# A decoder layer in FP32: regrouping the attention heads on the partitions, and who copies, casts and stores around them

## The chip, the core and the metric

One core of a Trainium2 chip runs the whole program. Its engines work side by side, each through its own list of instructions, and wait for one another at semaphores: TensorE (PE in the profile; PEld is its weight loading), VectorE (DVE), ScalarE (ACT), GpSimd (POOL), and SyncE (SP), which here only issues DMA transfers. The metric is the time of the program on the device in microseconds (us), the median of several runs.

## What is computed

A post-norm decoder layer for 8 sequences of 128 tokens, width 128, 16 heads of 8: self attention with learned relative position logits, causal cross attention, a routed mixture of 64 experts (8 chosen) with a shared expert; after each a residual and a layer norm.

```python
x = layernorm(x + attn(x, qkv_w, qkv_b, proj_w, proj_b, rel_emb))
#   logits = q k^T / sqrt(8) + pos,   pos[i, j] = q_i . rel_emb[j - i + 99], -1e8 outside
#   softmax, times v, times proj_w^T, + proj_b
x = layernorm(x + cross(x, ctx, wq, wk, wv, wo))      # the same without pos, causal
x = layernorm(x + routed(x) + relu2(x @ shared_up_w) @ shared_down_w)
#   routed: sigmoid scores, best 4 of 8 groups, best 8 experts, weights normed, x 2.5
#   each expert: relu(x @ up)^2 @ down
```

## The kernel before

**Preparation.** A list of tasks (`TASKS`) goes through seven PSUM banks in a ring: TensorE computes a task into a bank, ScalarE or VectorE (`by_vector`) copies it out, and only then may the task seven places later use the bank. The tasks transpose the weights and `x`, project queries and keys (`q0`, `q1`, `k0`, `k1`: halves of the tokens), transpose the relative embeddings (`rel`), make values (`v0`, `v1`) and the same of the context (`ctx0`, `ctx1`, `vc0`, `vc1`), then the router's weights, then 32 `bias` tasks of four products each (256 matmul records): for every query position one product of `rel_t` with `spread`, the queries laid out once per head through a mask (`spread_queries`, VectorE, four batches of 16 instructions, L1086; the mask is `head_mask`). They give the position logits `pos`. Last come the context's keys, `kc0` and `kc1`.

**High and low parts.** Scores are products of FP32 values split in two reduced parts each, high (`q_hi`, `k_hi`) and low (`q_lo`, and `k_t` after it is overwritten with its own low part). GpSimd makes both in halves of the tokens (L528 to L535). So that one matmul over 128 rows sums all four products of parts (high and low by high and low) of four heads with 8 dimensions each, SP stores the parts to DRAM (`keep`, L398) as often as they are needed, and `gather(B)` loads for sequence B (0 to 7 self attention, 8 to 15 cross attention) a stack of queries, `q_stk` (one DMA, L413), and a block-diagonal `k_bd` (four DMAs, one for each of the four heads, L417). Three stacks form a ring (`RING`); gather B waits until the scores of sequence B-3 are done, and in the cross attention also for the store of its own queries, `qc_kept`. Before, the features on the partitions are ordered by `(h d g)`: four blocks of heads `h`, 8 dimensions `d`, four groups `g` innermost. The store's DRAM tensor has the shape (4, 4 parts, 32, tokens).

**The pipeline.** From there each engine runs a loop over steps `s`, and each step does a piece of each stage. Attention is cut into 64 units U (16 sequences x 4 groups g; 32 and up are cross attention). `scores(U)` adds the logits (L700: `pos` transposed; L703: the causal mask) and the product L706; VectorE takes the negative maxima (L1123), ScalarE four exponentials (L916), TensorE transposes the probabilities two steps later (L718), then either VectorE (L1130) or ScalarE (L925) copies them, by `probs_by_vector(U)`, and TensorE multiplies with the values (L728). Output projection, residual, layer norm and the next queries follow at fixed distances. In steps 34 and 38 VectorE also splits the first two pieces of expert weights; GpSimd does the others, and SP loads them (`load_piece`).

The experts run as 68 steps k (k = s - 67): 34 for the first half of the tokens (two shared, 32 pairs of experts), 34 for the second. A step is three products up (L683, high and low parts), a `scaled` on VectorE (ReLU times the root of the expert's weight, L1262), two squares on ScalarE (L992, L993), a subtraction on GpSimd (`unit_lo`, L594), and four steps later three products down. The routing is cut into 14 parts for each of four batches of two sequences; `BATCHES` and `ROUTE0` say in which step which part goes onto VectorE. `CT` are the two steps in which TensorE turns the finished weights `root` (L796); ScalarE copies them out, SP stores them to `root_dram` and loads them back spread over 64 rows each (`roots`).

Of the kernel before, what the change touches and what calls it, by code (L numbers as in the profile page):

```python
# [21 lines left out]
H, HD = 16, 8  # L22
# [50 lines left out]
CT = [ROOTS_AT[1], ROOTS_AT[3] + 2]  # L73
# [48 lines left out]
def probs_by_vector(U):  # L122

    return U % 4 != 3 if U < NU else U % 2 == 0
# [13 lines left out]
def decoder_layer(nc, x, ctx_in, qkv_w, qkv_b, proj_w, proj_b, rel_emb, wq, wk, wv, wo,  # L138
                  router_w, corr, up_w, down_w, sh_up, sh_down, out):
    with ExitStack() as ctx:  # L140
# [30 lines left out]
        with ExitStack() as second:  # L171
# [125 lines left out]
        k_kept = [sem(f"k_kept{n}") for n in range(2)]  # L297
        q_kept = [sem(f"q_kept{n}") for n in range(2)]
# [74 lines left out]
        def _(sp):  # L373
# [21 lines left out]
            def keep(store, parts, cols, kept):  # L395

                for part, what in enumerate(parts):
                    sp.dma_start(store[:, part, :, cols], what[:, cols]).then_inc(kept, 16)  # L398

            def keep_queries(store, hi, lo, cols, kept):  # L400
                keep(store, (hi, lo, hi, lo), cols, kept)

            def keep_keys(store, hi, lo, cols, kept):
                keep(store, (hi, hi, lo, lo), cols, kept)

            def gather(B):
# [933 lines left out]
```

## Time and profile before

| | us |
|---|---|
| median of 3 runs | 346.91 |
| lowest, highest | 346.52, 347.46 |
| the profiled execution | 344.19 |
| its span | 342.4 |
| busy: PE, DVE, ACT, POOL | 267.5, 228.3, 207.3, 141.0 |

The span is the time between the first and the last instruction of the profiled execution. Busy times are sums over the span, of engines that work beside each other. In the timelines a row is one instruction or a run of like ones ("x16"), and the square brackets give the engine's idle time just before and what ended it.

### The profile page before, as it was taken

How to read it: one execution, taken by the hardware profiler on the slowest of the kernel's cores; microseconds unless marked ns; L12 is line 12 of the kernel's file. 1: busy time of each engine (PE TensorE's matmuls, PEld its weight loads, DVE VectorE, ACT ScalarE, POOL GpSimd, SP SyncE). 2: the span in 40 equal slices, each digit the busy share in tenths (PEclk: the TensorE clock that was granted, in tenths of full speed). 3: DMA queues.
4: the chain of work that ended last, by engine and by line, in shares of the span. 5: the costliest groups of instructions: out<-in, count | busy, mean ns of one | idle time of the engine just before them, and what ended most of it. 6: DMA issues, size and time to landing. Idle time of an engine off the chain costs nothing.

```text
span 342.4 us, 6024 instructions
## 1 busy us (share of the span) xinstructions
PE 267.5 (78%) x1904; PEld 210.6 (62%) x1904; DVE 228.3 (67%) x571; ACT 207.3 (61%) x573; POOL 141.0 (41%) x139
## 2 busy tenths in 40 slices
PE   2919999893069999998778775649969599999991
PEld 2608999572057887665555443538747488878870
DVE  2697854663038888986659989449999745674533
ACT  1502362774018888898767863346666578878861
POOL 7560000600000012244443500227569589879990
PEclk9976999998569999999989987688989899999997
DMA  6522225733432333465554100099547267658501
GB/s 113 144 97 104 102 103 180 172 83 130 154 105 64 94 94 92 93 158 149 149 167 136 50 0 3 15 225 253 138 124 171 73 163 179 174 160 215 142 0 31
DMA packets 55683, 41.09 MB, mean 120 GB/s; under 512 B 15394, under 2 KB 44772, under 8 KB 55652
## 3 DMA queue, kind: packets, MB, share of 16 engines
q1 hardware_dynamic: 55652, 40.71, 43.7%
q8 instruction: 15, 0.25, 0.3%
q14 instruction: 16, 0.13, 0.1%
HBM read 31.52 MB, written 9.18 MB: 119 GB/s over the span
## 4 chain that ended last, share of the span: by engine, by line
PE 41%; DVE 18%; SPq 12%; DMA 11%; issue 7%; POOL 5%; ACT 4%; POOLq 0%; DVEq 0%; ACTq 0%
PE bank L683 14%; PE bank L667 9%; SPq L417 6%; DMA qc_dram<-q_lo 5%; POOL unit_lo L594 5%; PE bank L718 4%; PE bank L700 4%; DVE spread L1086 3%; SPq L398 2%; DMA k_bd<-k_dram 2%; SPq L413 2%; PE bank L728 2%; DVE scaled L1262 2%; PE bank L706 2%; PE bank L739 1%
## 5 line engine op out<-in xcount | busy, mean ns | idle before, releaser
L594 POOL TENSOR_TENSOR unit_lo<-unit,unit_hi 128x512 fp32r<-128x512 f32 x68 | 87.3, 1303 | 48.7 <-ACT unit_hi L993 47.5
L916 ACT ACTIVATE probs<-bank,neg_max 128x128 f32<-128x128 f32 x256 | 72.3, 390 | 29.1 <-DVE neg_max L1123 28.1
L1262 DVE SCALAR_TENSOR_TENSOR scaled<-bank,roots 128x512 f32<-128x512 f32 x64 | 43.4, 686 | 30.2 <-PE bank L683 22.5
L1123 DVE TENSOR_REDUCE neg_max<-bank 128x4 f32<-128x512 f32 x64 | 42.9, 683 | 29.6 <-PE bank L706 29.0
L992 ACT ACTIVATE unit<-scaled 128x512 f32<-128x512 f32 x68 | 42.7, 628 | 32.8 <-DVE scaled L1262 30.5
L718 PE MATMUL bank<-ident,probs 128*128 128x128 f32 x256 | 39.9, 279 | 3.3 <-DVE probs_t L1130 2.4
L993 ACT ACTIVATE unit_hi<-scaled 128x512 fp32r<-128x512 f32 x68 | 41.9, 616 | 0.0
L718 PEld LDWEIGHTS bank<-ident,probs 128*128 128x128 f32 x256 | 30.5, 145 | 10.5 <-issue 5.2
L561 POOL CAST q_hi<-q_t 128x128 fp32r<-128x128 f32 x8 | 2.3, 293 | 83.6 <-ACT q_t L963 83.6
L706 PE MATMUL bank<-k_bd,q_stk 128*128 128x512 f32 x64 | 34.6, 540 | 0.0
L1130 DVE COPY probs_t<-bank 128x512 f32<-128x512 f32 x40 | 27.5, 687 | 10.4 <-PE bank L718 9.7
L700 PE MATMUL bank<-ident,pos 128*128 128x128 f32 x128 | 20.5, 283 | 17.4 <-DMA k_bd<-k_dram 17.4
L683 PE MATMUL bank<-unit_hi,w_hi 128*128 128x512 f32 x64 | 26.6, 415 | 3.8 <-POOL unit_lo L594 3.8
L667 PE MATMUL bank<-spread,rel_t 128*128 128x128 f32 x256 | 29.3, 278 | 0.0
L1086 DVE TENSOR_SCALAR spread<-q_t,head_mask 128x256 f32<-128x256 f32 x64 | 25.0, 466 | 6.3 <-ACT q_t L883 3.3
L667 PEld LDWEIGHTS bank<-spread,rel_t 128*128 128x128 f32 x256 | 29.1, 194 | 0.1
L700 PEld LDWEIGHTS bank<-ident,pos 128*128 128x128 f32 x128 | 14.6, 143 | 21.4 <-issue 19.9
L683 PE MATMUL bank<-x_hi,w_hi 128*128 128x512 f32 x64 | 26.6, 415 | 0.1
L683 PE MATMUL bank<-x_hi,w_lo 128*128 128x512 f32 x64 | 25.9, 405 | 0.0
L683 PE MATMUL bank<-unit_lo,w_hi 128*128 128x512 f32 x64 | 25.7, 401 | 0.0
L683 PE MATMUL bank<-x_lo,w_hi 128*128 128x512 f32 x64 | 25.7, 401 | 0.0
L683 PE MATMUL bank<-unit_hi,w_lo 128*128 128x512 f32 x64 | 25.6, 400 | 0.0
(176 smaller groups left out, 480.6 us busy)
## 6 DMA issues: line engine op xcount, KB each, us to landing
roots<-root_dram SPq DMA_DIRECT2D x64, 256.0 KB, 4.6
q_stk<-q_dram SPq DMA_DIRECT2D x8, 256.0 KB, 3.6
k_bd<-k_dram SPq DMA_DIRECT2D x32, 64.0 KB, 3.0
incoming<-in_L_ffn_up_w SPq DMA_DIRECT2D x4, 512.0 KB, 5.3
q_stk<-qc_dram SPq DMA_DIRECT2D x8, 256.0 KB, 3.0
k_bd<-kc_dram SPq DMA_DIRECT2D x32, 64.0 KB, 2.4
incoming<-in_L_ffn_down_w SPq DMA_DIRECT2D x4, 512.0 KB, 4.8
q_dram<-q_hi SPq DMA_DIRECT2D x4, 256.0 KB
```

What stands on the lines that cost most here:

```text
L594: nc.gpsimd.tensor_tensor(unit_lo[:, k % R], unit[:, k % 3], unit_hi[:, k % R], ALU.subtract).then_inc(lo_ready, 1)
L667: last = nc.tensor.matmul(bank_of(f"bias{n}")[:, m * 128:(m + 1) * 128], rel_t[:, L - 1 - i:2 * L - 1 - i], q_spread[:, i // 32 % 2, i % 3 ...
L683: ins = nc.tensor.matmul(bank, w[a], act[b], start=(first and n == 0), stop=(last and n == 2), skip_group_check=True)
L700: nc.tensor.matmul(bank[:, h4 * L:(h4 + 1) * L], pos[:, row, :], ident[:, :], start=(h4 == 0), stop=False, is_transpose=True, skip_group_c ...
L706: nc.tensor.matmul(bank[:, :], q_stk[r][:, g, :], k_bd[r][:, g].rearrange("p h j -> p (h j)"), start=False, stop=True, skip_group_check=Tr ...
L718: last = nc.tensor.transpose(ps[BP][:, h4 * L:(h4 + 1) * L], probs[:, U % 3, h4 * L:(h4 + 1) * L], ident[:, :])
L916: last = nc.scalar.activation(probs[:, U % 3, h4 * L:(h4 + 1) * L], ps[BS[U % 3]][:, h4 * L:(h4 + 1) * L], ACT.Exp, bias=neg_max[:, U % 4, ...
L992: nc.scalar.activation(unit[:, k % 3], scaled[:, k % 3], ACT.Square)
L993: nc.scalar.activation(unit_hi[:, k % R], scaled[:, k % 3], ACT.Square).then_inc(hi_ready, 1)
L1086: last = nc.vector.tensor_scalar(q_spread[:, c % 2, :, h * NB:(h + 1) * NB], src, head_mask[:, h:h + 1], None, ALU.mult)
L1123: nc.vector.tensor_reduce(neg_max[:, U % 4, :], ps[BS[U % 3]][:, :].rearrange("p (h j) -> p h j", h=GH), AX.X, ALU.max, negate=True).then_ ...
L1262: ins = nc.vector.scalar_tensor_tensor(scaled[:, k % 3], h, 0.0, roots[:, n % ROOT_RING, c % ROOTS], ALU.max, ALU.mult)
```

## The change

- **Order of features.** On the partitions the heads are now innermost: `(d h)`, 8 dimensions by 16 heads. Weights, biases, relative embeddings and the head mask are permuted to that. `k_bd` rows of one head are every fourth partition (`h4::GH`) instead of 32 in a row.
- **Stores.** `keep` stores a part as 128 plain rows. Queries are stored once for the high and once for the low part (before: twice each), keys still twice each. The self attention's stores are no longer in halves of the tokens. A gather loads the query stack in two DMAs of 64 rows.
- **Order on SP.** Gather 2 comes ahead of the two first pieces of weights; the stores of the context's keys come after gathers 3 and 4 instead of ahead of gather 3.
- **High parts.** ScalarE makes `q_hi` and `k_hi` of the self attention, all tokens in one instruction each, ahead of its copies of the bias tasks. GpSimd waits for the first two batches of `spread`, then subtracts.
- **Probabilities.** In the cross attention VectorE copies one unit in four, ScalarE three; before, each copied two.
- **Routing.** The third batch of two sequences takes 12 steps instead of 8, the fourth starts at step 84 instead of 80; the weights of the second half are turned at step 96 instead of 93, one step after the last part of the routing instead of two.

```diff
-BATCHES = [(range(0, 2), 2), (range(2, 4), 3.5), (range(4, 6), 1.75), (range(6, 8), 1.2)]
+BATCHES = [(range(0, 2), 2), (range(2, 4), 3.5), (range(4, 6), 1.2), (range(6, 8), 1.2)]
 ROUTE0 = [NG * (NB + seqs[-1]) + M + USE + 2 for seqs, _ in BATCHES]
+ROUTE0[3] += NG
...
-CT = [ROOTS_AT[1], ROOTS_AT[3] + 2]
+CT = [ROOTS_AT[1], ROOTS_AT[3] + 1]
...
-    return U % 4 != 3 if U < NU else U % 2 == 0
+    return U % 4 != 3 if U < NU else U % 4 == 0
...
-        q_dram, k_dram, qc_dram, kc_dram = (
-            nc.dram_tensor(f"{n}_dram", (GH, REPS, HD * NG, NB * L), F32, kind="Internal").ap()
-            for n in ("q", "k", "qc", "kc"))
+        q_dram, qc_dram = (nc.dram_tensor(f"{n}_dram", (2, D, NB * L), F32, kind="Internal").ap() for n in ("q", "qc"))
+        k_dram, kc_dram = (nc.dram_tensor(f"{n}_dram", (REPS, D, NB * L), F32, kind="Internal").ap() for n in ("k", "kc"))
...
-            def keep(store, parts, cols, kept):
-
-                for part, what in enumerate(parts):
-                    sp.dma_start(store[:, part, :, cols], what[:, cols]).then_inc(kept, 16)
-
-            def keep_queries(store, hi, lo, cols, kept):
-                keep(store, (hi, lo, hi, lo), cols, kept)
-
-            def keep_keys(store, hi, lo, cols, kept):
-                keep(store, (hi, hi, lo, lo), cols, kept)
+            def keep(store, parts, what, cols, kept):
+
+                for part in parts:
+                    sp.dma_start(store[part, :, cols], what[:, cols]).then_inc(kept, 16)
...
-                sp.dma_start(q_stk[r][:, :, :].bitcast(F32),
-                             queries[:, :, :, cols].rearrange("h s (d g) t -> (h s d) g t", g=NG))\
-                    .then_inc(stack_here[r], 16)
+                for rep in range(2):
+                    sp.dma_start(q_stk[r][rep * 64:(rep + 1) * 64, :, :].bitcast(F32),
+                                 queries[:, :, cols].rearrange("s (d h g) t -> (s d h) g t", h=GH, g=NG))\
+                        .then_inc(stack_here[r], 16)
                 for h4 in range(GH):
-                    sp.dma_start(k_bd[r][ROWS * h4:ROWS * (h4 + 1), :, h4, :].bitcast(F32),
-                                 keys[h4, :, :, cols].rearrange("s (d g) t -> (s d) g t", g=NG))\
+                    sp.dma_start(k_bd[r][h4::GH, :, h4, :].bitcast(F32),
+                                 keys[:, :, cols].rearrange("s (d h g) t -> h (s d) g t", h=GH, g=NG)[h4])\
                         .then_inc(stack_here[r], 16)
...
-            for f in range(2):
-                cols = slice(f * HT, (f + 1) * HT)
-                sp.wait_ge(q_split, 2 * (f + 1))
-                keep_queries(q_dram, q_hi, q_lo, cols, q_kept[f])
-                sp.wait_ge(k_split, 2 * (f + 1))
-                keep_keys(k_dram, k_hi, k_t, cols, k_kept[f])
+            sp.wait_ge(q_high, 1)
+            keep(q_dram, (0,), q_hi, every, q_kept)
+            sp.wait_ge(k_high, 1)
+            keep(k_dram, (0, 1), k_hi, every, k_kept)
+            sp.wait_ge(q_split, 1)
+            keep(q_dram, (1,), q_lo, every, q_kept)
+            sp.wait_ge(k_split, 1)
+            keep(k_dram, (2, 3), k_t, every, k_kept)
...
             sp.wait_ge(zeroed, 3)
+            gather(2)
             load_piece(0)
             load_piece(1)
-            gather(2)
...
-            sp.wait_ge(k_split, 6)
-            keep_keys(kc_dram, k_hi, kc_t, slice(0, NB * L), kc_kept)
             for B in range(RING, 2 * NB):
...
                 gather(B)
+                if B == RING:
+                    sp.wait_ge(k_split, 3)
+                    keep(kc_dram, (0, 1), k_hi, every, kc_kept)
+                if B == RING + 1:
+                    keep(kc_dram, (2, 3), kc_t, every, kc_kept)
...
-                    keep_queries(qc_dram, q_hi, q_lo, slice(b * L, (b + 1) * L), qc_kept[b % 2])
+                    keep(qc_dram, (0,), q_hi, cols, qc_kept[b % 2])
+                    keep(qc_dram, (1,), q_lo, cols, qc_kept[b % 2])
...
+            pool.wait_ge(spread_ready, 2)
+            pool.wait_ge(q_high, 1)
+            nc.gpsimd.tensor_tensor(q_lo[:, :].bitcast(F32R), q_t[:, :], q_hi[:, :], ALU.subtract).then_inc(q_split, 1)
+            pool.wait_ge(k_high, 1)
+            nc.gpsimd.tensor_tensor(k_t[:, :].bitcast(F32R), k_t[:, :], k_hi[:, :], ALU.subtract).then_inc(k_split, 1)
...
+            act.wait_ge(out_a, out_count("k1", False))
+            nc.scalar.copy(q_hi[:, :].bitcast(F32R), q_t[:, :]).then_inc(q_high, 1)
+            nc.scalar.copy(k_hi[:, :].bitcast(F32R), k_t[:, :]).then_inc(k_high, 1)
```

How the instructions stand, at three places. SP around gathers 2 to 4, before (rows by 128-wide patterns; `x2` is a run):

```order
L413 DMA q_stk<-q_dram 128x4x128
L417 DMA k_bd<-k_dram 32x4x128 x4
L426 DMA incoming<-in_L_ffn_up_w 128x16x64 x2
L413 DMA q_stk<-q_dram 128x4x128
L417 DMA k_bd<-k_dram 32x4x128 x4
L398 DMA kc_dram<-k_hi 4x32x1024 x2
L398 DMA kc_dram<-k_t 4x32x1024 x2
L413 DMA q_stk<-q_dram 128x4x128
L417 DMA k_bd<-k_dram 32x4x128 x4
```

And the same place now, from gather 2 on:

```order
L410 DMA q_stk<-q_dram 64x4x128 x2
L414 DMA k_bd<-k_dram 32x4x128 x4
L423 DMA incoming<-in_L_ffn_up_w 128x16x64 x2
L410 DMA q_stk<-q_dram 64x4x128 x2
L414 DMA k_bd<-k_dram 32x4x128 x4
L400 DMA kc_dram<-k_hi 128x1024 x2
L410 DMA q_stk<-q_dram 64x4x128 x2
L414 DMA k_bd<-k_dram 32x4x128 x4
L400 DMA kc_dram<-k_t 128x1024 x2
```

Gather 3 now stands ahead of all stores of the context's keys, and these have an outer dimension of 128 rows instead of 4 blocks.

GpSimd after its masks and zeros, before, where the `spread` of VectorE runs:

```order
L528 CAST q_hi<-q_t 128x512
L530 TENSOR_TENSOR q_lo<-q_t,q_hi 128x512
L533 CAST k_hi<-k_t 128x512
L535 TENSOR_TENSOR k_t<-k_t,k_hi 128x512
L528 CAST q_hi<-q_t 128x512
L530 TENSOR_TENSOR q_lo<-q_t,q_hi 128x512
L533 CAST k_hi<-k_t 128x512
L535 TENSOR_TENSOR k_t<-k_t,k_hi 128x512
L542 TENSOR_TENSOR x_tok<-x_tok,pb_row 128x1024
```

And now, where the first of them waits for two batches of `spread`:

```order
L530 TENSOR_TENSOR q_lo<-q_t,q_hi 128x1024
L532 TENSOR_TENSOR k_t<-k_t,k_hi 128x1024
L538 TENSOR_TENSOR x_tok<-x_tok,pb_row 128x1024
L541 MEMSET k_bd 128x2048
L544 CAST k_hi<-k_t 128x1024
```

The four casts are gone from GpSimd; the subtractions are two, of the same total size, and start later.

ScalarE in the cross attention, one sequence (four units), before:

```order
L942 ACTIVATE ln_var<-moments,eps_col 128x1
L943 ACTIVATE rstd<-ln_var 128x1
L916 ACTIVATE probs<-bank,neg_max 128x128 x4
L931 COPY o_t<-bank 128x512
L937 COPY on_t<-bank 128x128
L963 COPY q_t<-bank 128x128
L925 COPY probs_t<-bank 128x512
L916 ACTIVATE probs<-bank,neg_max 128x128 x8
L955 COPY x_t<-bank 128x128
L925 COPY probs_t<-bank 128x512
L916 ACTIVATE probs<-bank,neg_max 128x128 x4
```

And now:

```order
L938 ACTIVATE ln_var<-moments,eps_col 128x1
L939 ACTIVATE rstd<-ln_var 128x1
L912 ACTIVATE probs<-bank,neg_max 128x128 x4
L927 COPY o_t<-bank 128x512
L933 COPY on_t<-bank 128x128
L959 COPY q_t<-bank 128x128
L921 COPY probs_t<-bank 128x512
L912 ACTIVATE probs<-bank,neg_max 128x128 x4
L921 COPY probs_t<-bank 128x512
L912 ACTIVATE probs<-bank,neg_max 128x128 x4
L951 COPY x_t<-bank 128x128
L921 COPY probs_t<-bank 128x512
```

One more copy of probabilities stands between two sets of exponentials.

## Rows read from the trace of the kernel before

**Rows 1.** Timeline of VectorE: start us, us, line, operation, out<-in, count [idle before].

```profile
12.24 12.11 DVE L1086 TENSOR_SCALAR spread<-q_t,head_mask 128x256 f32<-128x256 f32 x16 [3.27 <-ACT q_t L883]
...
25.81 4.28 DVE L1086 TENSOR_SCALAR spread<-q_t,head_mask 128x256 f32<-128x256 f32 x16
```

**Rows 2.** Stretches, L1086 alone: length, busy (instructions), granted clock, DMA share, GB/s.

```profile
12.20:22.40 10.20, 10.16 (x9) 0.94 0.29 86
22.40:24.30 1.90, 1.90 (x8) 0.50 0.26 102
```

**Rows 3.** Timeline of TensorE at the start.

```profile
24.74 1.11 PE L611 MATMUL bank<-ident,ctx_tok 128*128 128x128 f32 x4 [7.98 <-DVE rel_t L1105]
26.53 3.78 PE L623 MATMUL bank<-wc_t,ctx_t 128*128 128x128 f32 x16 [0.68 <-ACT ctx_t L896]
```

**Rows 4.** The bias loop in the chain, and a stretch of it for all engines.

```profile
30.61 29.22 PE bank L667 x256
...
40.50:59.80 19.30, 19.30 (x175) 19.30 (x174) 10.74 (x31) 9.10 (x16) 0.00 (x0) 1.00 0.40 137
```

**Rows 5.** Waits over the whole run: in total, times, longest.

```profile
PE bank L700 <- DMA k_bd<-k_dram: 17.4, 1, 17.4
...
PE bank L703 <- DMA k_bd<-kc_dram: 8.7, 5, 2.4
...
PE bank L796 <- DVE root L1239: 7.9, 2, 4.3
```

**Rows 6.** Timeline of SP's queue: the time that issuing took.

```profile
70.76 6.27 SPq L398 DMA_DIRECT2D kc_dram<-k_t  x2
77.07 4.99 SPq L413 DMA_DIRECT2D q_stk<-q_dram  x1
```

**Rows 7.** Stretches: length, busy PE, PEld, DVE, ACT, POOL, clock, DMA share, GB/s.

```profile
27.30:47.90 20.60, 20.60 (x167) 20.26 (x166) 14.24 (x43) 7.69 (x14) 0.00 (x0) 0.90 0.27 103
226.30:236.00 9.70, 5.98 (x23) 5.04 (x24) 8.52 (x30) 7.07 (x19) 5.64 (x5) 0.82 1.04 241
```

**Rows 8.** The chain's DMA steps from issue to landing, and SP issuing four loads.

```profile
147.75 3.96 DMA qc_dram<-q_lo
...
218.92 2.27 DMA root_dram<-q_lo
...
152.34 2.55 SPq L417 DMA_DIRECT2D k_bd<-kc_dram  x4
```

**Rows 9.** Stretches as in rows 7: cross attention, its end, experts.

```profile
136.51:151.00 14.49, 13.23 (x138) 9.00 (x134) 12.98 (x28) 12.98 (x48) 4.13 (x7) 1.00 0.49 115
151.00:182.35 31.35, 24.55 (x241) 17.48 (x237) 21.02 (x46) 24.90 (x91) 17.08 (x14) 0.95 0.54 153
182.35:205.40 23.05, 16.92 (x159) 11.14 (x159) 20.74 (x74) 16.87 (x62) 5.46 (x7) 0.93 0.20 56
226.30:271.20 44.90, 34.23 (x135) 26.27 (x136) 41.52 (x121) 28.61 (x62) 31.38 (x27) 0.92 0.67 169
271.20:333.60 62.40, 61.40 (x267) 49.84 (x267) 33.55 (x56) 50.09 (x90) 54.97 (x43) 0.98 0.55 142
```

**Rows 10.** Timeline of ScalarE: one copy of probabilities in the cross attention.

```profile
149.06 0.64 ACT L925 COPY probs_t<-bank 128x512 f32<-128x512 f32 x1
```

**Rows 11.** Timeline of GpSimd: an addition over 1024 columns.

```profile
19.97 2.39 POOL L542 TENSOR_TENSOR x_tok<-x_tok,pb_row 128x1024 f32<-128x1024 f32 x1
```

**Rows 12.** Timeline of TensorE: the score products of units 9, 13, 33 and 56.

```profile
75.51 0.48 PE L706 MATMUL bank<-k_bd,q_stk 128*128 128x512 f32 x1
...
101.21 0.48 PE L706 MATMUL bank<-k_bd,q_stk 128*128 128x512 f32 x1
...
136.51 0.58 PE L706 MATMUL bank<-k_bd,q_stk 128*128 128x512 f32 x1
...
182.35 0.58 PE L706 MATMUL bank<-k_bd,q_stk 128*128 128x512 f32 x1
```

**Rows 13.** The page's group of that line: busy, mean ns, idle before.

```profile
L1262 DVE SCALAR_TENSOR_TENSOR scaled<-bank,roots 128x512 f32<-128x512 f32 x64 | 43.4, 686 | 30.2 <-PE bank L683 22.5
```

More of the change, by code:

```diff
@@ L296, in decoder_layer @@
         qc_split = sem("qc_split")
-        k_kept = [sem(f"k_kept{n}") for n in range(2)]
-        q_kept = [sem(f"q_kept{n}") for n in range(2)]
+        k_kept = sem("k_kept")
+        q_kept = sem("q_kept")
+        q_high = sem("q_high")
+        k_high = sem("k_high")
         qc_kept = [sem(f"qc_kept{n}") for n in range(2)]
@@ L523, in _ @@
             nc.gpsimd.memset(glist[:, :, TOPG:8], -3.0e38).then_inc(consts_made, 1)
-            for f in range(2):
-                cols = slice(f * HT, (f + 1) * HT)
-                pool.wait_ge(out_a, out_count(f"q{f}", False))
-                nc.gpsimd.tensor_copy(q_hi[:, cols].bitcast(F32R), q_t[:, cols]).then_inc(q_split, 1)
-                pool.wait_ge(q_split, 2 * f + 1)
-                nc.gpsimd.tensor_tensor(q_lo[:, cols].bitcast(F32R), q_t[:, cols], q_hi[:, cols], ALU.subtract)\
-                    .then_inc(q_split, 1)
-                pool.wait_ge(out_a, out_count(f"k{f}", False))
-                nc.gpsimd.tensor_copy(k_hi[:, cols].bitcast(F32R), k_t[:, cols]).then_inc(k_split, 1)
-                pool.wait_ge(k_split, 2 * f + 1)
-                nc.gpsimd.tensor_tensor(k_t[:, cols].bitcast(F32R), k_t[:, cols], k_hi[:, cols], ALU.subtract)\
-                    .then_inc(k_split, 1)
+            pool.wait_ge(spread_ready, 2)
[3 more added lines that the diff above has]
+            nc.gpsimd.tensor_tensor(k_t[:, :].bitcast(F32R), k_t[:, :], k_hi[:, :], ALU.subtract).then_inc(k_split, 1)
             pool.wait_ge(ld["x0"], 16)
@@ L546, in _ @@
             pool.wait_ge(out_a, sum(not by_vector(t) for t in TASKS))
-            for f in range(2):
-                pool.wait_ge(k_kept[f], 16 * REPS)
+            pool.wait_ge(k_kept, 16 * REPS)
             nc.gpsimd.tensor_copy(k_hi[:, :].bitcast(F32R), kc_t[:, :]).then_inc(k_split, 1)
-            pool.wait_ge(k_split, 5)
+            pool.wait_ge(k_split, 2)
             nc.gpsimd.tensor_tensor(kc_t[:, :].bitcast(F32R), kc_t[:, :], k_hi[:, :], ALU.subtract).then_inc(k_split, 1)
@@ L558, in _ @@
                     if b == 0:
-                        for f in range(2):
-                            pool.wait_ge(q_kept[f], 16 * REPS)
+                        pool.wait_ge(q_kept, 16 * 2)
                     nc.gpsimd.tensor_copy(q_hi[:, cols].bitcast(F32R), q_t[:, cols]).then_inc(qc_split, 1)
@@ L694, in scores @@
                 if g == 0:
[L695 removed]
+                    pe.wait_ge(stack_here[r], 16 * (2 + GH) * (B // RING + 1))
                 if U < NU:
@@ L890, in _ @@
             for c in range(2):
-                nc.scalar.copy(wc_t[:, c, :].rearrange("p (h d g) -> p h d g", h=GH, g=NG),
-                               done("w_cross")[:, c * D:(c + 1) * D].rearrange("p (h g d) -> p h d g", h=GH, g=NG))
+                nc.scalar.copy(wc_t[:, c, :].rearrange("p (d h) -> p h d", h=H),
+                               done("w_cross")[:, c * D:(c + 1) * D].rearrange("p (h d) -> p h d", h=H))
             nc.scalar.copy(wc_t[:, 2:4, :].rearrange("p c d -> p (c d)"), done("w_cross")[:, 2 * D:4 * D])\
@@ L904, in _ @@
                                    done(f"bias{n}").rearrange("p (i r) -> p r i", i=4)).then_inc(out_a, 1)
-            for f in range(2):
-                act.wait_ge(k_kept[f], 16 * REPS)
+            act.wait_ge(k_kept, 16 * REPS)
             nc.scalar.mul(kc_t[:, 0:HT], done("kc0"), SCALE).then_inc(out_a, 1)
@@ L1069, in _ @@
             dve.wait_ge(ld["rel"], 16)
[L1070 to L1071 removed]
+            nc.vector.tensor_copy(rel_perm[:, 0, :].rearrange("p (d h) -> p h d", h=H),
+                                  rel_raw[:, 0, :].rearrange("p (h d) -> p h d", h=H))
             dve.wait_ge(ld["rel2"], 16)
[L1073 to L1074 removed]
+            nc.vector.tensor_copy(rel_perm[:, 1, :].rearrange("p (d h) -> p h d", h=H),
+                                  rel_raw[:, 1, :].rearrange("p (h d) -> p h d", h=H))\
                 .then_inc(rel_ordered, 1)
```

31 lines of the change are left out of this document (12 added, 19 removed).

## Prediction

> **What bounds the kernel now.** I read the chain of waits first, then the longest waits by line, then the timeline around each of them. No engine bounds the whole; four places do.
>
> The start. The first 16 `spread` instructions of VectorE take 12.11 us, the next 16, same shape, 4.28 us [rows 1]. Until 22.4 us GpSimd subtracts and adds beside them and 9 of them touch that stretch; in the 1.90 us after it 8 go through [rows 2]. So the cost is the company, not the work. `rel_t` stands behind them on VectorE, TensorE waits 7.98 us for it, and then runs `vc0`/`vc1` in 3.78 us [rows 3], still near the granted clock of 0.50, 1.2 GHz, to which it fell while TensorE stood idle [rows 2]. Only then does the loop of 128 bias products start, 29.22 us long [rows 4].
>
> The hole. TensorE waits 17.4 us for `k_bd`, once [rows 5]: gather 3 stands on SP behind four `kc_dram` stores, whose second pair takes 6.27 us to issue and whose backlog holds the next `q_stk` issue for 4.99 us [rows 6]. While SP only stores, 0.27 of the 16 DMA engines are busy and 103 GB/s move; with `roots` loads 1.04 and 241 GB/s [rows 7]. 0.27 of 16 is four engines, and the stored pattern's outer dimension is four (4x32x1024 in the order of SP above).
>
> The cross attention. From unit 41 on, TensorE waits for `k_bd<-kc_dram`, 8.7 us in all [rows 5]; the chain there is five issues of loads, four of stores, and the landing of the last store, 3.96 us from its issue [rows 8].
>
> The experts' first part. From 226.3 to 271.2 us VectorE is busy 41.52 of 44.9 us, TensorE 34.23; after it TensorE is busy 61.40 of 62.4 [rows 9].
>
> **The change, part by part**, against the profiled execution: 344.19 us, of which the span is 342.4.
>
> *Start.* GpSimd now waits for the first 32 spreads, and its casts are ScalarE's. The first 16 spreads then cost 4.28 instead of 12.11: from 12.24 to 16.52. The two small `rel_t` copies kept TensorE until 0.39 us after the spreads (24.35 to 24.74), so `ctx1` starts at 16.9. From it to the start of `vc0` were 1.79 us at half clock (24.74 to 26.53); say 1.3. Then `vc0`/`vc1` half of their 3.78 us, 1.9, at full clock, 2.4 GHz, since TensorE is now idle for about 1 us instead of 8, and 0.4 for the router: the bias loop starts at 20.6, not 30.6. At the full clock 175 records took 19.30 us, so 256 take 28.2 [rows 4], and it ends at 48.8 against 59.83: **11.0 us**. Ends: 7.8 us if only the spreads gain, 11.4 if the three small steps vanish too.
>
> What this costs in cover: ScalarE does two 128x1024 casts, some 1.3 us each by two copies of 0.64 [rows 10], at about 21 to 23.5 us; its first bias copy is due at 27, so they are hidden. GpSimd does two subtractions and the `x_tok` addition, 3 x 2.39 [rows 11], from about 23 to 30. The third batch of spreads starts when bias task 7 is done, at 27.6, so up to 2.4 us of it is slowed as at the start. It would end near 34 and is needed at bias 16, 34.7. That margin is thin; without it TensorE waits a microsecond or two. The stores start at 22.5 rather than 14, 3 MB instead of 4 MB. On 16 engines at the 241 GB/s of the loads [rows 7] they need 12.5 us, and two gathers 4 us more: some 42 us, before the scores start at about 50.7.
>
> *Hole.* Gather 2 goes ahead of the two pieces, gather 3 ahead of the `kc_dram` stores, and these run on 16 engines, half before gather 4 and half after. Gather 3 can be issued when unit 3 is scored (about 54 us) and its data come behind gather 2 and two pieces, 1.5 MB, 6 to 8 us: there by about 63, needed at 68. So nothing replaces the wait. Unit 9 to unit 13 took 25.70 us [rows 12]. Units 13 to 33 took 35.30 us, 7.06 for four, so the hole costs 25.70 - 7.06 = **18.6 us**, of which 1.2 is what follows the 17.4 us wait, at a lowered clock. If gather 3 or 4 is late after all, I allow 3.6 us: 15 to 18.6.
>
> *Cross attention.* Four loads take 2.55 us to issue, 0.64 each. SP's round was eight issues and then 3.96 us from the last one to its landing, 9.1 us; it becomes seven issues and a landing, for which the nearest row is `root_dram`, a plain store, 2.27 us [rows 8]: 6.8 us for four units. The units took 8.4 (31.35 us for 15, units 41 to 56) [rows 9]. So SP no longer sets the pace; next is ScalarE. Undisturbed, units 33 to 41 took 14.49 us, 7.24 for four, with ScalarE busy 12.98 of it [rows 9]. It gets one more copy for four units, 0.64 us at most, and has 0.76 us idle. I take 7.4, nearest to the undisturbed row, because a copy in the step fills what ScalarE waits for VectorE's maxima. Units 33 to 56 took 45.84 us [rows 12]; 23 units at 7.4/4 are 42.55: **3.3 us**. Ends: 4.2 (the pace stays 7.24) and 0.8 (the copy adds all of its 0.6).
>
> *End of the attention*, 182.35 to 205.4 us: VectorE is busy 20.74 of 23.05 us [rows 9], with the first routing in it. Two of its copies go, 1.2 us, and a part of the last DMA wait: **1.9 us**, between 0.5 and 3.
>
> *Routing of the second half.* It is spread over 24 steps instead of 20, and the weights are turned at step 96 instead of 93. Its work stays. While VectorE sets the pace, three more steps pass at the cost of a `scaled`, 0.69 us [rows 13], rather than of TensorE's step, 6 products of 0.23 = 1.38 us (61.40 us for 267) [rows 9]: 3 x 0.69 = **2.1 us**. The turn comes one step sooner after its routing; TensorE waits for `root` twice today, 7.9 us in all [rows 5], and may wait a step more: -1.5. If TensorE is never held up in the three steps: 4.1. The new `roots` are due seven steps after the turn, 9.7 us, and take store and load, about 9: just hidden.
>
> The regrouped heads change access patterns, not sizes, in instructions off these chains: nothing. The sum is 11.0 + 18.6 + 3.3 + 1.9 + 2.1 = 36.9 us: 344.19 - 36.9 = 307.3 for a profiled execution. The median of the runs is 2.72 above the profiled one, so **310.0 us**. All low ends together give 324.3, all high ends 305.6.
>
> **Two pages.** The four engines of [rows 7] are what the Trainium skill states in "DMA: Bandwidth & Descriptors", section on why a DMA increments its semaphore by 16: the number of engines is the largest one up to 16 that divides the slowest dimension of both patterns. By that rule the new stores get 16.
>
> Against the change speaks "SBUF — State Buffer" of the Trainium skill, section on the DMA port swizzle: 64 rows reach the same eight ports as 32, so each half of the new `q_stk` load would move at half the rate of the whole. What it would do here is rival C.
>
> **The rivals.**
> A. ScalarE bounds the cross attention. For it: it is busy 12.98 of 14.49 us. Against it: its idle time is larger than the copy. Then the third and fourth term are nothing: 310.0 + 5.2 = 315.2 us. Chance 0.15.
> B. The stores are bound by memory, not by four engines: 103 GB/s stays. Then 3 MB end at 52 instead of 35, the first scores wait 8 us, and `kc_dram` takes 20 us as now, though behind gather 3: 318 to 322. Against it: the 0.27. Chance 0.05.
> C. The two 64-row loads each last as long as the one 128-row load did, 1 to 1.5 us more in a round. In the self attention two gathers of lead hide it. In the cross attention SP's round is then 6.8 + 1.5 = 8.3 again and the third term and a part of the fourth are lost: 314. Chance 0.07.
> D. VectorE's spreads are slow for another reason than GpSimd (the stores beside them): the first term is gone, 321. Against it: [rows 2] changes within the store stream, at the moment GpSimd ends. Chance 0.03.
> E. The other side: the loads with new strides back up. If each `q_stk` half held SP as long as the one after the stores, 4.99 us [rows 6], a gather would take 12.5 us against the 7.06 of four units, and 14 gathers would add over 70 us: slower than before. It decides from 7.06 + 36.9/14 = 9.7 us a gather on. Against it: both outer dimensions, 64 and 32, fill 16 engines. Chance 0.01.
>
> **How the numbers follow.** The forecast has 0.69. A and C lie inside a range to 318; below, I go to 303 for what gets better by itself without stalls. That leaves out B, D, E and a part of the forecast's edges. About 0.3% (1 us) can be told from no change here. All cases but E are faster by far more: faster 0.98, same 0.01, slower 0.01.
>
> **What would show it.** Right: sixteen spreads in 4.3 us at 12.2; the bias loop from about 20.6 to 48.8; no gap before unit 12; granted clock 1.00 there; a DMA share far over 0.27 in the stores; rounds of 7.2 to 7.5 us for four units in the cross attention with no wait for `k_bd`; the second turn of weights behind 29 expert steps. Wrong: a bias loop that waits for the third batch of spreads, a wait for `k_bd` at units 0, 12 or 16, ScalarE over 7.8 us for four cross units, or TensorE waiting for the second set of `roots`.

## The result, and the profile after

| | before, us | after, us |
|---|---|---|
| median | 346.72 | 310.1 |
| lowest, highest | 345.05, 347.46 | 309.06, 310.34 |
| the profiled execution | 344.19 | 310.34 |
| its span | 342.4 | 308.6 |
| busy: PE, DVE, ACT, POOL | 267.5, 228.3, 207.3, 141.0 | 263.7, 217.3, 210.9, 138.0 |

The ratio is 0.8944, with a 95% interval of 0.8906 to 0.8982. Of all executions reported here one, of `half_copies` below (316.22 us), fell in the chip's slower state, and it is left out of that kernel's median and ratio. The forecast was 310.0 us. That it is met to 0.1 us is partly luck, as the stretches show. A unit counts from its score product, and "the first unit with roots" from the first `scaled` of the experts that uses loaded `roots`. The stretches follow one another without a gap, and their differences add up to that of the two spans.

| stretch of the profiled execution | before | after | gain | forecast |
|---|---|---|---|---|
| start to the first score product (unit 0) | 61.75 | 52.47 | 9.3 | 11.0 |
| unit 0 to 9 | 13.76 | 13.75 | 0.0 | 0 |
| unit 9 to 13 (the hole) | 25.70 | 6.79 | 18.9 | 18.6 |
| unit 13 to 33 | 35.30 | 35.27 | 0.0 | 0 |
| unit 33 to 56 (cross attention) | 45.84 | 40.51 | 5.3 | 3.3 |
| unit 56 to the first unit with roots | 43.92 | 40.41 | 3.5 | 1.9 |
| from there to the end | 116.1 | 119.4 | -3.3 | 2.1 |
| sum | 342.4 | 308.6 | 33.8 | 36.9 |

The sum of the forecast was 3 us too high. The profiled execution of before lies 2.5 us below its median, that of after 0.2 us above its own, and I had carried the offset over to the changed kernel; the two errors cancel.

**The start.** Timeline of VectorE after the change (columns as in [rows 1]):

```profile
12.45 4.29 DVE L1080 TENSOR_SCALAR spread<-q_t,head_mask 128x256 f32<-128x256 f32 x16 [2.88 <-ACT q_t L877]
...
18.19 4.29 DVE L1080 TENSOR_SCALAR spread<-q_t,head_mask 128x256 f32<-128x256 f32 x16
...
29.23 5.27 DVE L1080 TENSOR_SCALAR spread<-q_t,head_mask 128x256 f32<-128x256 f32 x16 [0.28 <-PE bank L661]
```

Sixteen spreads take 4.29 us where they took 12.11 [rows 1]. The third batch, which begins beside GpSimd's addition to `x_tok`, takes 1 us more, and TensorE never waits for it. TensorE, where [rows 3] stood:

```profile
19.52 2.05 PE L617 MATMUL bank<-wc_t,ctx_t 128*128 128x128 f32 x16 [1.01 <-ACT ctx_t L890]
...
21.71 28.52 PE L661 MATMUL bank<-spread,rel_t 128*128 128x128 f32 x253
```

The same 16 matmuls take 2.05 instead of 3.78 us, and the bias loop starts at 21.7 instead of 30.6.

**The hole.** SP's queue now (as [rows 6]), and a stretch of the stores (as [rows 7]):

```profile
62.00 2.56 SPq L414 DMA_DIRECT2D k_bd<-k_dram  x4
64.60 1.06 SPq L400 DMA_DIRECT2D kc_dram<-k_hi  x2
65.70 2.01 SPq L410 DMA_DIRECT2D q_stk<-q_dram  x2
```

```profile
23.30:31.00 7.70, 7.70 (x72) 7.70 (x71) 6.28 (x10) 2.13 (x4) 7.00 (x3) 1.00 0.91 370
```

While SP stores, 0.91 of the 16 DMA engines are busy and 370 GB/s move, against 0.27 and 103 [rows 7]. The stores hold SP no longer: two of 512 KB take 1.06 us to issue. The loads around them still queue a little (2.99 us for the two halves of a `q_stk` at 58.96 us, against 1.21 us later on), but no score product waits for it. The score products of units 9, 13, 33 and 56 (as [rows 12]) stand at

```profile
66.22 0.48 PE L700 MATMUL bank<-k_bd,q_stk 128*128 128x512 f32 x1
...
73.01 0.48 PE L700 MATMUL bank<-k_bd,q_stk 128*128 128x512 f32 x1
...
108.28 0.59 PE L700 MATMUL bank<-k_bd,q_stk 128*128 128x512 f32 x1
...
148.79 0.58 PE L700 MATMUL bank<-k_bd,q_stk 128*128 128x512 f32 x1
```

**The rest.** Stretches as in [rows 9]: cross attention in two parts, its end, the experts up to the second turn of weights and behind it:

```profile
108.28:122.50 14.22, 13.21 (x137) 9.01 (x134) 13.01 (x30) 13.24 (x48) 4.12 (x7) 1.00 0.48 107
122.50:148.79 26.29, 23.93 (x240) 16.55 (x237) 19.47 (x40) 25.30 (x94) 17.38 (x14) 1.00 0.65 171
148.79:171.84 23.05, 17.13 (x168) 11.43 (x165) 20.95 (x93) 19.36 (x70) 5.09 (x6) 0.97 0.16 46
189.20:239.90 50.70, 37.99 (x153) 29.05 (x153) 44.38 (x125) 32.89 (x70) 36.65 (x31) 0.92 0.60 149
239.90:299.70 59.80, 58.82 (x248) 47.53 (x248) 30.90 (x52) 45.57 (x82) 49.70 (x39) 0.95 0.60 148
```

Units 41 to 56 now take 26.29 us instead of 31.35, with ScalarE busy 25.30 of them. That is not yet a bound: `half_copies` below takes the same time with ScalarE busy 23.87. The chain that ended last leads from 121.95 to 134.13 us through SP's issues and the landings behind them, and after that through ScalarE and VectorE in turn. The second turn of weights comes 50.7 us behind the first unit with roots, three steps later than before, where it came after 44.9. The waits that answer to [rows 5], over the whole run:

```profile
PE bank L790 <- DVE root L1233: 9.2, 2, 5.3
...
PE bank L697 <- DMA k_bd<-kc_dram: 0.9, 2, 0.6
```

TensorE waits 0.9 us for `k_bd<-kc_dram` (2.5 in the second profile of the same kernel, the yardstick below), where it was 8.7, and never for `k_bd<-k_dram`. For `root` it waits longer than before, 9.2 us instead of 7.9, with 5.3 at the second turn.

### The profile page after: what moved, and what is told of

The parts are those of the page before. It is cut to its first block, busy times and chain, and to the rows that moved or that the text cites. A ratio compares the mean times of both kernels' runs of the same rounds, so it can differ in the third digit from the quotient of the medians.

```text
span 308.6 us, 6010 instructions
## 1 busy us (share of the span) xinstructions
PE 263.7 (85%) x1904; PEld 206.3 (67%) x1904; DVE 217.3 (70%) x563; ACT 210.9 (68%) x583; POOL 138.0 (45%) x133
## 4 chain that ended last, share of the span: by engine, by line
PE 48%; DVE 12%; POOL 11%; ACT 9%; issue 8%; DMA 5%; SPq 5%; POOLq 1%; DVEq 0%; ACTq 0%
PE bank L677 16%; POOL unit_lo L588 10%; PE bank L661 9%; PE bank L712 5%; PE bank L694 4%; ACT probs L912 4%; SPq L414 2%; PE bank L722 2%; PE bank L610 2%; PE bank L700 2%; PE bank L733 2%; DMA roots<-root_dram 1%; SPq L410 1%; DMA qc_dram<-q_lo 1%; PE bank L617 1%
## 5 line engine op out<-in xcount | busy, mean ns | idle before, releaser
L912 ACT ACTIVATE probs<-bank,neg_max 128x128 f32<-128x128 f32 x256 | 73.7, 407 | 5.0 <-DVE neg_max L1117 4.0
L712 PE MATMUL bank<-ident,probs 128*128 128x128 f32 x256 | 39.0, 275 | 3.9 <-DVE probs_t L1124 1.8
L712 PEld LDWEIGHTS bank<-ident,probs 128*128 128x128 f32 x256 | 29.1, 140 | 11.1 <-issue 5.8
L1124 DVE COPY probs_t<-bank 128x512 f32<-128x512 f32 x32 | 22.0, 688 | 7.8 <-PE bank L712 7.1
L921 ACT COPY probs_t<-bank 128x512 f32<-128x512 f32 x32 | 20.4, 636 | 6.8 <-PE bank L712 6.8
L1080 DVE TENSOR_SCALAR spread<-q_t,head_mask 128x256 f32<-128x256 f32 x64 | 18.1, 361 | 5.0 <-ACT q_t L877 2.9
L722 PE MATMUL bank<-probs_t,v_aug 128*9 128x128 f32 x512 | 20.4, 278 | 0.0
```

What stands on the lines that cost most here:

```text
L712: last = nc.tensor.transpose(ps[BP][:, h4 * L:(h4 + 1) * L], probs[:, U % 3, h4 * L:(h4 + 1) * L], ident[:, :])
L722: last = nc.tensor.matmul(ps[BO][32 * h4:32 * h4 + NV, g * L:(g + 1) * L], v_aug[:, B // NB, B % NB, head_of(g, h4), :], probs_t[:, U % 3, ...
L912: last = nc.scalar.activation(probs[:, U % 3, h4 * L:(h4 + 1) * L], ps[BS[U % 3]][:, h4 * L:(h4 + 1) * L], ACT.Exp, bias=neg_max[:, U % 4, ...
L1124: nc.vector.tensor_copy(probs_t[:, U % 3, :], ps[BP][:, :]).then_inc(pt_out_v, 1)
```

## The experiments

Four questions: are four DMA engines what made the stores slow; what is the order on SP worth without them; what do the copies do; and where did the experts lose 3.3 us? `after_again`, `old_routing`, `late_turn` and `half_copies` ran on one chip, the other eight on a second one, in two groups of four: `four_engines`, `order_alone`, `old_order` and `quiet_spread`, then the rest. A ratio is always to the kernel before on the same chip and in the same group. A stretch is compared from its own start, because the bias loop begins anywhere from 20.1 to 21.7 us in executions of kernels that do not differ up to there.

### The yardstick

> The changed kernel once more, unedited, on the chip on which the three edits of it are timed. 310.1 us; its spread is the yardstick for them.

308.82 us (307.32 to 310.29), ratio 0.8945 (0.891 to 0.898), the same as the first time.

### Stores on four engines

```diff
                 for part in parts:
-                    sp.dma_start(store[part, :, cols], what[:, cols]).then_inc(kept, 16)
+                    sp.dma_start(store[part, 0:124, cols], what[0:124, cols]).then_inc(kept, 16)
+                    sp.dma_start(store[part, 124:128, cols], what[124:128, cols]).then_inc(kept, 16)
```

> The changed kernel with every store of high and low parts cut into 124 rows and 4 rows; both numbers have 4 as their largest divisor up to 16, the data and the order are the same. Theory 1 (four engines bound the stores of before): the DMA share falls to 0.27 and 103 GB/s in the stores; 3 MB take 30 us from 23.5 on, so the first scores start at about 60 instead of 52.5, a wait for k_bd comes back near unit 16 or 20 behind kc_dram (20 us for 2 MB), and the cross attention slows toward 8 us for four units: 8 to 20 us slower than the changed kernel. Rival (memory or the store's total bytes bound it): nothing changes but some 0.5 us of issues, 310 to 312.

336.44 us (335.88 to 337.0), ratio 0.9731 (0.9687 to 0.9775): 26 us above the changed kernel, beyond the 8 to 20 that I expected, but by the mechanism of theory 1. The same bytes in the same order, with a row count whose largest divisor up to 16 is four. The stretch from the first store on (as [rows 7]), then the waits:

```profile
23.00:62.00 39.00, 28.74 (x247) 27.44 (x245) 18.69 (x46) 12.29 (x21) 11.29 (x6) 0.94 0.25 91
```

```profile
PE bank L695 <- DMA k_bd<-k_dram: 19.8, 3, 11.9
```

The DMA share is 0.25, four engines of 16. A busy engine moves about as much in each kernel: 91 GB/s over 4.0 engines are 23 GB/s, 103 over 4.3 are 24 [rows 7], 370 over 14.6 are 25. So the stores of before were short of engines, and rival B, a bound by memory, does not fit. The first score product comes at 64.4 instead of 52.4 us (12.0), units 0 to 33 take 68.4 instead of 55.8 (12.5), units 33 to 63 take 55.9 instead of 53.8 (2.1). My estimate missed most of the second piece: gather 4 and 5 come late too, behind either pair of `kc_dram` stores.

The same kernel says something on the cross attention. Units 41 to 56 take 27.56 us with stores on four engines, 26.3 with all 16 and 31.35 before, and on the chain the last store of queries lands after 2.30 us, 1.70 and 3.96 [rows 8]. For four engines a stretch and the chain's step, then the chain's step of the changed kernel:

```profile
147.00:174.56 27.56, 23.39 (x240) 16.67 (x237) 19.24 (x39) 25.62 (x94) 16.93 (x14) 1.00 0.57 159
...
151.76 2.30 DMA qc_dram<-q_lo
```

```profile
125.84 1.70 DMA qc_dram<-q_lo
```

So only 1.3 of the 5 us won there need the 16 engines. The other 3.8 are there without them. The obvious candidate is that queries are now stored once instead of twice, which halves the bytes ahead of that landing, but no run takes this back by itself.

### The order on SP, alone and taken back

In `order_alone` the kernel before gets the order of the changed kernel:

```diff
...
+            gather(2)
             load_piece(0)
             load_piece(1)
-            gather(2)
...
-            sp.wait_ge(k_split, 6)
-            keep_keys(kc_dram, k_hi, kc_t, slice(0, NB * L), kc_kept)
...
                 gather(B)
+                if B == RING:
+                    sp.wait_ge(k_split, 6)
+                    keep(kc_dram, (k_hi, k_hi), slice(0, NB * L), kc_kept)
+                if B == RING + 1:
+                    keep2(kc_dram, (kc_t, kc_t), slice(0, NB * L), kc_kept)
```

`keep2` is `keep` for the last two of the four parts.

> The kernel before with one edit: SP's order of the changed kernel (gather 2 ahead of the pieces, gather 3 ahead of the kc_dram stores, these in two pairs behind gathers 3 and 4), stores still on four engines. Theory 1 (order and speed both make the hole): the wait moves from unit 12 to unit 16 or 20 and shrinks by the time that the pipeline had work: 17.4 us become 5 to 12, 335 to 341 in all. Rival (order alone made it): no wait, 329. Rival (speed alone): 17 us still, 346.

335.17 us (334.96 to 335.38), ratio 0.9694 (0.9666 to 0.9722). The wait moved to units 16 and 20 and became smaller:

```profile
PE bank L708 <- DMA k_bd<-k_dram: 8.3, 3, 4.7
```

In `old_order` the changed kernel gets the order of before:

```diff
-            gather(2)
             load_piece(0)
             load_piece(1)
+            gather(2)
+            sp.wait_ge(k_split, 3)
+            keep(kc_dram, (0, 1), k_hi, every, kc_kept)
+            keep(kc_dram, (2, 3), kc_t, every, kc_kept)
...
-                if B == RING:
-                    sp.wait_ge(k_split, 3)
-                    keep(kc_dram, (0, 1), k_hi, every, kc_kept)
-                if B == RING + 1:
-                    keep(kc_dram, (2, 3), kc_t, every, kc_kept)
```

> The changed kernel with SP's order of before around gathers 2 and 3 (pieces, gather 2, four kc_dram stores, gather 3), stores on 16 engines. Theory 1 (speed of the stores is what matters): 2 MB need 8 us or less instead of 20, gather 3 comes in at about 70 where unit 12 wants it at 70.5: 0 to 3 us slower than the changed kernel. Rival (order is what matters): a wait for k_bd of over 6 us at unit 12.

310.26 us (310.06 to 310.45), ratio 0.8973 (0.8947 to 0.8999). Unit 12 is scored at 70.51 us, in the changed kernel (yardstick) at 70.44. So the speed of the stores alone closes the hole. The order alone takes half of it (units 0 to 33 take 65.5 us instead of 74.8, where the changed kernel takes 55.8), and on fast stores it brings nothing that can be measured.

### GpSimd held back, on the kernel before

```diff
+            pool.wait_ge(spread_ready, 2)
             for f in range(2):
                 cols = slice(f * HT, (f + 1) * HT)
                 pool.wait_ge(out_a, out_count(f"q{f}", False))
```

> The kernel before with one edit: GpSimd waits for the first two batches of spread before it casts and subtracts. Theory 1: the first 16 spreads take 4.3 us instead of 12.1, and the bias loop starts near 21.5 and ends near 50.4 instead of 59.8. But the stores, 4 MB on four engines at 103 GB/s, then start at about 24.5 and need 40 us, so the first scores start no earlier than about 66 to 70 and the hole behind kc_dram stays: slower than before by 4 to 10 us. Rival (the spreads are slow because of the stores beside them): they take 12 us still.

354.34 us (354.13 to 354.56), ratio 1.0249 (1.0219 to 1.0278): slower, as expected. VectorE:

```profile
12.15 4.29 DVE L1087 TENSOR_SCALAR spread<-q_t,head_mask 128x256 f32<-128x256 f32 x16 [2.13 <-ACT q_t L884]
```

One wait on GpSimd makes the 16 spreads three times as fast. By itself this does not put rival D out, since the stores wait for GpSimd's parts and so move away from the spreads as well, from 14.15 to 24.23 us. What does is the second batch of the kernel before, as a stretch: 16 spreads in 4.28 us with GpSimd idle and the stores running at 103 GB/s.

```profile
25.81:30.10 4.29, 3.61 (x17) 3.49 (x16) 4.28 (x17) 1.17 (x2) 0.00 (x0) 0.50 0.26 103
```

The bias loop of `quiet_spread` begins at 20.35 us. But the stores start 10 us later and still run on four engines, so TensorE waits for the first gather and then again for gather 3, 14.46 us where it was 17.4:

```profile
71.83 1.09 PE L701 MATMUL bank<-ident,pos 128*128 128x128 f32 x4 [19.72 <-DMA k_bd<-k_dram]
...
105.69 1.08 PE L701 MATMUL bank<-ident,pos 128*128 128x128 f32 x4 [14.46 <-DMA k_bd<-k_dram]
```

So this part of the change is a loss alone, and is worth something only with faster stores.

### The copies of before in the cross attention

```diff
-    return U % 4 != 3 if U < NU else U % 4 == 0
+    return U % 4 != 3 if U < NU else U % 2 == 0
```

> The changed kernel with the copies of before in the cross attention (two of four by VectorE). Theory 1: with SP no longer in the way the pace there is that of the undisturbed stretch of before, 7.24 us for four units, where the changed kernel shows 7.05, and the end of the attention gets 1.2 us more on VectorE: 2 to 3 us slower than the changed kernel, 312 to 313. Theory 2: the faster stores alone made the cross attention faster, the copies are off the path: 310.1. Theory 3 (the prediction's term): ScalarE's extra copy costs time in the cross attention, 7.4 against 7.24 for four units, so this one is faster in that stretch by 1 us.

312.97 us (310.95 to 314.84), ratio 0.9066 (0.9025 to 0.9108). The yardstick's three stretches (units 33 to 41, 41 to 56, 56 to 63), and those of this kernel, columns as in [rows 9]:

```profile
108.19:122.46 14.27, 13.02 (x137) 9.11 (x134) 13.07 (x30) 13.29 (x49) 4.17 (x7) 1.00 0.49 109
122.46:148.71 26.25, 23.59 (x240) 16.58 (x237) 19.00 (x39) 25.36 (x94) 17.26 (x14) 1.00 0.63 170
148.71:162.03 13.32, 12.30 (x130) 8.35 (x127) 12.77 (x58) 13.16 (x49) 5.19 (x7) 1.00 0.27 77
```

```profile
106.70:121.18 14.48, 13.23 (x137) 9.00 (x134) 13.06 (x28) 12.96 (x48) 4.13 (x7) 1.00 0.52 114
121.18:147.49 26.31, 24.05 (x241) 16.29 (x237) 21.30 (x47) 23.87 (x88) 17.39 (x14) 1.00 0.61 164
147.49:162.85 15.36, 12.61 (x130) 8.20 (x127) 13.47 (x58) 12.27 (x46) 5.11 (x6) 1.00 0.25 70
```

Theories 1 and 2 hold in one stretch each, the third in none. From unit 41 to 56 it makes no difference who copies (26.25 and 26.31): the gain of 5 us there comes from the rest of the change, stores and loads. Before unit 41, where VectorE also splits weights, three copies on ScalarE save 0.2 us; from unit 56, where the routing begins, 2.0 us, and another 0.9 between unit 63 and the first unit with roots (27.7 against 26.8). That ScalarE's extra copy costs time is seen nowhere. In the experts this profiled execution is 1.0 us shorter than the yardstick's, with the same code. So the profiled executions account for about 2 of the 4.2 us between the medians; the profiled one is the fastest of this kernel's, and where the others lose the rest is open.

### The routing of the second half

Five kernels vary two things: the routing of before (20 steps) or the stretched one (24), and in which step TensorE turns the second half's weights. The shortest and the longest edit:

```diff
-CT = [ROOTS_AT[1], ROOTS_AT[3] + 1]
+CT = [ROOTS_AT[1], ROOTS_AT[3] + 2]
```

```diff
-BATCHES = [(range(0, 2), 2), (range(2, 4), 3.5), (range(4, 6), 1.2), (range(6, 8), 1.2)]
+BATCHES = [(range(0, 2), 2), (range(2, 4), 3.5), (range(4, 6), 1.75), (range(6, 8), 1.2)]
...
-ROUTE0[3] += NG
...
-CT = [ROOTS_AT[1], ROOTS_AT[3] + 1]
+CT = [ROOTS_AT[1], ROOTS_AT[3] + 5]
```

> The changed kernel with the routing schedule of before (third batch in 8 steps, fourth from step 80, weights turned at step 93, two steps after the last part). From the first routed unit to the end the changed kernel took 119.4 us and the one before 116.1. Theory 1: the new schedule costs that, because TensorE waits 5.3 us for root at a turn one step after its last part and then runs at a lowered clock: about 3.3 us faster than the changed kernel, 306.8. Theory 2: the schedule brings the 2.1 us of the prediction and the loss comes from elsewhere: 312.2, and the stretch grows to 121.5.

> As old_routing, but the weights of the second half are turned five steps after the last part of the routing (step 96, as in the changed kernel). Theory 1: TensorE's wait for root at the turn (3.6 us before, 5.3 now) is real time and was paid because the turn stood too close behind VectorE's last part; five steps of products cover it, and the clock stays up: another 3 to 4 us, 303 to 304. Rival: VectorE's backlog sets the pace there, and what TensorE does not wait at the turn it waits at the next scaled: as old_routing, 306.8.

> The changed kernel with the weights of the second half turned at step 97 instead of 96, two steps after the last part of its (stretched) routing. Theory 1 (the distance from VectorE's last part to the turn costs, the stretched schedule itself does not): TensorE's wait for root at that turn falls from 5.9 to 4.5 us or less, 1 to 2 us faster than the changed kernel: about 308. Theory 2 (the stretched schedule costs by itself): as the changed kernel.

> The same at step 99, four steps after the last part: TensorE should not wait for root at the turn at all. But from the turn to the first loaded roots are 8.8 us, six and a half steps, and the first expert of the second half is due four steps after step 99. Theory 1: 5.9 us are saved at the turn and 2 to 4 come back as a wait of VectorE for roots, with TensorE idle behind it: 306 to 308, no better than the stretched schedule at 97. Rival: the wait for roots is hidden by the two shared units and the lag of VectorE: 304 to 305.

> The changed kernel with the routing of before, but its turn at step 92, one step after the last part, as in the changed kernel, not two. Theory 1 (distance to the turn): TensorE waits 5 to 6 us for root there instead of 3.6 at step 93, and the kernel lies 1 to 2 us above the one that turns at 93, near 308.5, that is at the changed kernel. Theory 2 (the stretch itself costs): as with the turn at 93, 306.5 to 307.

> The kernel with the routing of before and its turn five steps after the last part (step 96) once more, beside the three others: 304 to 306, 1% under the changed kernel, no wait for root at the second turn.

The table has, for the profiled executions, the time from the first unit with roots to the end, and TensorE's wait for `root` at the second turn.

| kernel | routing | turn, distance | to the end, us | wait, us | median, us | ratio |
|---|---|---|---|---|---|---|
| before | 20 steps | 93, 2 | 116.1 | 3.6 | | 1 |
| changed (`after_again`) | 24 | 96, 1 | 119.7 | 5.9 | 308.82 | 0.8945 |
| `old_routing` | 20 | 93, 2 | 116.6 | 3.6 | 307.27 | 0.8899 (0.8865 to 0.8932) |
| `late_turn` | 20 | 96, 5 | 114.9 | 0 | 305.95 | 0.8852 (0.8819 to 0.8885) |
| `stretched_97` | 24 | 97, 2 | 117.8 | 4.6 | 307.4 | 0.887 (0.882 to 0.8919) |
| `stretched_99` | 24 | 99, 4 | 117.5 | 0.6 | 310.84 | 0.8945 (0.8877 to 0.9014) |
| `turn_92` | 20 | 92, 1 | 117.6 | 5.0 | 308.8 | 0.8912 (0.8859 to 0.8964) |
| `late_turn_again` | 20 | 96, 5 | 114.5 | 0 | 304.0 | 0.8777 (0.8713 to 0.8841) |

With the routing of before the loss is gone (116.6 against 116.1). In these profiles both theories have a part. At the same distance of one step the stretched routing is 2.1 us longer than the other (119.7 and 117.6), of two steps 1.2 us (117.8 and 116.6). And from distance one to two the stretch becomes 1.0 (20 steps) or 1.9 us (24 steps) shorter, from two to five another 1.9 (average of two).

How far this carries: each stretch is that of one profiled execution, and three profiles of code that is alike there (`after`, `after_again`, `old_order`) have 119.4, 119.7 and 119.5 us, but `half_copies`, alike as well, has 118.7. So differences of 1 to 2 us are near the scatter. The medians show less: `old_routing` lies 1.6 us below the changed kernel on the same chip, with intervals that overlap, and its ratio does not differ from that of `stretched_97` (0.8899 and 0.887), so the cost of the stretched routing by itself is not shown by them. Clear of noise is `late_turn` against the changed kernel. It was expected at 303 to 304 us, though, 3 to 4 us below `old_routing`, and lies 1.3 us below it.

The clock has a part in it (the granted clock of TensorE, where 1.00 is 2.4 GHz and 0.50 is 1.2 GHz). In the yardstick TensorE stands idle for 5.94 us ahead of its turn at 240.01, and in the 10 us behind it the granted clock is 0.72 and 35 of its matmuls fit; in `late_turn` the turn takes 0.60 us at 236.96 without a wait, and 42 fit. The rows behind their turns, the yardstick's two first:

```profile
240.01:245.20 5.19, 5.19 (x15) 4.12 (x16) 1.24 (x2) 2.44 (x5) 1.27 (x1) 0.50 0.12 28
240.00:250.00 10.00, 9.99 (x35) 8.03 (x36) 3.32 (x5) 5.61 (x10) 4.52 (x4) 0.72 0.52 121
```

```profile
237.00:247.00 10.00, 8.86 (x42) 7.17 (x41) 5.15 (x8) 9.67 (x19) 9.62 (x8) 1.00 0.25 66
```

Seven matmuls at 0.23 us are 1.6 us on top of the wait, as an estimate. In the kernels of the table, waits of 3.6 to 5.9 us ahead of the turn left the clock at 0.50 (its first four matmuls take 1.06 us in `old_routing`); the wait of 0.6 us in `stretched_99` did not (0.63 us).

`stretched_99` shows the opposite risk. The turn waits only 0.6 us, but VectorE waits for the `roots` that are loaded after it:

```profile
DVE scaled L1256 <- DMA roots<-root_dram: 6.9, 3, 4.9
```

Its stretch is only 0.3 us shorter than with the turn at 97, and the profiled execution is the fastest of four: the median is 3.4 us longer (310.84 against 307.4), beyond the 306 to 308 that were expected. What the other three lose is open. The routing of before leaves room on both sides of a turn at step 96: five steps ahead of it and seven behind it, where VectorE's wait for the new `roots` is 0.8 us (`late_turn`). `late_turn` is the fastest of its group, with 0.8852 against 0.8945 for the changed kernel on the same chip, 1.0% faster, and `late_turn_again` the fastest of its own.

## Why the prediction was right, point by point

- **Start: right in kind, 1.7 us high** (9.3 to the first score, 11.0 forecast). The spreads' 4.28 us and the matmuls at full clock came as worked out; the steps in front of the loop took longer (it starts at 21.7 instead of 20.6) and the loop 28.5 instead of 28.2. In other executions, of kernels alike up to there, it starts as early as 20.1, so about 1 us of it is not the kernel's. The thin margin of the third batch held, with 1 us of slowing instead of 2.4.
- **Hole: right** (18.9 for 18.6). That four engines were the cause is shown by the 124-row stores. Order alone takes half of the hole (`order_alone`), and none of it is lost when it is taken back on fast stores (`old_order`). I had given order and speed no shares; they are not additive, and speed alone does it.
- **Cross attention: right that SP's round set the pace, size too low** (5.3 for 3.3). The step that was mis-sized is the pace after it, 7.4 us for four units, from the stretch that I took for "undisturbed". 14.49 us for units 33 to 41 included VectorE's splitting of weights; the pace behind it is 26.29/15 x 4 = 7.0 us, not 7.4. SP's round is as forecast or better: from 121.35 to 127.56 us in SP's timeline are 6.2 us against 6.8, with a last landing of 1.70 us where I took 2.27. That ScalarE comes next did not hold: `half_copies` has the same 26.3 us with one copy less on ScalarE. That puts rival A out. Rival C is out as well: the wait for `k_bd<-kc_dram` is 0.9 us, 2.5 in the yardstick.
- **End of the attention: right, a little low** (3.5 for 1.9). `half_copies` gives 2.0 + 0.9 us of it to the copies, by one profile each, more than the 1.2 us of their bare durations.
- **Routing: wrong in sign** (-3.3 for +2.1, outside its own ends of -1.5 and 4.1). The step that failed: "While VectorE sets the pace, three more steps pass at the cost of a `scaled`". VectorE did not set it throughout: it is busy 44.38 of 50.70 us, where it was 41.52 of 44.9 [rows 9]. Stretching the routing opened gaps on VectorE rather than closing them on TensorE, and 5.8 us went by for three steps, 1.7 of them the longer wait for `root` (5.3 instead of 3.6). On top, I priced the turn's shorter distance as a step more of waiting, and left out the clock behind the wait.
- **B** is out with a share of 0.91 and 370 GB/s; **E** too: the six loads of a gather are issued in 3.8 us, and in 5.6 at most beside the pieces, where 9.7 us would have been needed. **D** is out by the second batch of spreads of before.
- **The sum** was 36.9 for 33.8 of spans; the offset between a profiled execution and the median, 2.7 before, is 0.2 after. A single profiled execution can stand anywhere among the runs, and such an offset should not be carried over as a constant.

On the page that spoke against the change: by the port swizzle section of "SBUF — State Buffer" in the Trainium skill the two halves of `q_stk` should move at half rate. The trace does not agree with a cost: a half of 128 KB lands after 3.2 us (median), the whole of 256 KB took 3.0 to 3.6 us before, and two halves are issued in 1.21 us. A `k_bd` load of 64 KB lands after 2.5 us, so at these sizes the landing depends little on the bytes, and no stretch with gathers became longer.

## What to carry to other kernels

If DMA share times 16 is a small whole number while a queue does nothing but store, look at the outer dimension of the stored pattern: here a layout on the partitions that lets both the stores and the loads have 128, 64 or 32 as outer dimension was worth more than all other parts together: taking the 16 engines back lost 26 of 37 us. Before an engine is held back for the sake of another, look at what waits behind it: quieting GpSimd alone made the kernel 2.5% slower, since the stores behind it then became the wait. And place a hand-over between engines by distance from its producer, not by the calendar: TensorE's turn of weights wants several steps behind VectorE's last part and enough steps ahead of the loads that follow, and a stall of TensorE of several us is paid a second time at the lower clock.

## What the runs showed of the hardware

- Stores from 128 rows ran at 370 GB/s with 0.91 of the engines busy; the same data as 124 + 4 rows at 91 GB/s with 0.25, as 4x32 rows at 103 GB/s with 0.27. By "DMA: Bandwidth & Descriptors" in the Trainium skill, in its section on why a DMA increments its semaphore by 16, the number of engines is the largest one up to 16 that divides the slowest dimension of both patterns. The trace agrees for 124 rows, which only happen to be divisible by four: 0.25 of 16 is four.
- A `tensor_scalar` of 256 columns on VectorE takes 0.27 us alone, and 9 of them spread over 10.2 us beside GpSimd's casts, subtractions and addition; GpSimd's own addition over 1024 columns takes 2.39 us beside them and 2.35 to 2.41 us elsewhere.
- TensorE idle for 5.9 us was followed by 10 us at a granted clock of 0.72 on average, 0.50 (1.2 GHz) for the first 5.2 us of it.
